# A fourth tile of attention features, new forms of the transfers that fill it, and an earlier second batch

## What is computed

```
mod = (silu(c) @ wmod) -> sa, ca, ga, sb, cb, gb      # per batch; ga, gb: size at least 0.25
h   = layernorm(x) * (1 + ca) + sa
q, k, v = split(h @ qkv_w.T + qkv_b);  q, k = rope(q), rope(k)
attn = softmax(causal(q k^T / sqrt(8)));  o = attn v
x = x + ga * (o @ proj_w.T + proj_b)
h = layernorm(x) * (1 + cb) + sb
y = relu(h @ W_fc.T)^2 @ W_proj.T
x = x + gb * spikes(y) / 5        # how many of 5 thresholds y is over
```

## Time and profile before

| | |
|---|---|
| device time, median of 3 runs | 444.27 us (440.36 to 444.5) |
| the profiled execution | 443.15 us |
| its span (first to last instruction) | 441.4 us |
| TensorE busy / VectorE busy / ScalarE busy | 390.9 / 329.3 / 256.8 us |
| mean granted TensorE clock, share of full speed | 0.988 |

### The profile page before, as it was taken

The page is one execution under the profiler, slowest core; times in us unless marked ns, Lnnn a source line. Parts: engine busy times, 40 slices in busy tenths (PEclk is TensorE's granted clock), DMA queues, the critical chain, the costliest instruction groups (busy, mean ns, idle before and its releaser), DMA issues.

```text
span 441.4 us, 15622 instructions
## 1 busy us (share of the span) xinstructions
PE 390.9 (89%) x6599; PEld 253.1 (57%) x6599; DVE 329.3 (75%) x730; ACT 256.8 (58%) x447; POOL 126.1 (29%) x163
## 2 busy tenths in 40 slices
PE   2778899888999989998899999998998889988885
PEld 2327555555656755666457654765566646753653
DVE  6659995886886988878986997699866777541176
ACT  8203465565676756765666665766665457566523
POOL 6714310430343043503342234304330220040020
PEclk9989999999999999999999999999999899998999
DMA  7056363243314233242415251323233050011001
GB/s 214 22 161 169 99 218 88 70 116 102 104 45 119 75 101 93 80 122 49 137 50 139 64 138 48 117 72 99 67 113 86 16 146 6 25 45 27 3 1 49
DMA packets 26050, 38.53 MB, mean 87 GB/s; under 512 B 5796, under 2 KB 20716, under 8 KB 23692
## 3 DMA queue, kind: packets, MB, share of 16 engines
q1 hardware_dynamic: 25980, 37.53, 29.8%
HBM read 26.35 MB, written 8.65 MB: 79 GB/s over the span
## 4 chain that ended last, share of the span: by engine, by line
PE 41%; DMA 18%; DVE 13%; ACT 10%; POOL 6%; issue 5%; SPq 5%; ACTq 0%; POOLq 0%; DVEq 0%
PE o_bank L611 10%; DMA kf<-k_scr 9%; PE d_bank L528 7%; DVE negmax L978 6%; PE t_bank L593 6%; PE s_bank L548 5%; DMA rden<-r_scr 4%; ACT probs L827 4%; PE a_bank L528 3%; DMA r_scr<-rden_c 2%; POOL parts L1303 2%; PE s_bank L528 2%; SPq L440 2%; PE t_bank L528 2%; POOL o_n L1325 2%
## 5 line engine op out<-in xcount | busy, mean ns | idle before, releaser
L978 DVE TENSOR_REDUCE negmax<-s_bank 128x1 f32<-128x512 f32 (+7 forms) x368 | 192.9, 566 | 56.9 <-PE s_bank L554 54.6
L827 ACT ACTIVATE probs<-t_bank 128x512 f32<-128x512 f32 x288 | 163.0, 594 | 89.8 <-PE t_bank L598 84.5
L548 PE MATMUL s_bank<-kf,qf 126*64 126x512 bf16 (+7 forms) x1024 | 118.7, 293 | 11.8 <-DMA kf<-k_scr 6.2
L593 PE MATMUL t_bank<-qf,kf 128*64 128x512 bf16 (+7 forms) x1024 | 113.3, 290 | 10.8 <-ACT probs L827 9.8
L611 PE MATMUL o_bank<-probs,v 128*32 128x512 f32 (+7 forms) x1024 | 75.1, 412 | 0.0
L548 PEld LDWEIGHTS s_bank<-kf,qf 126*64 126x64 bf16 x1024 | 50.6, 111 | 40.6 <-DVE negmax L978 19.9
L554 PE MATMUL s_bank<-causal,identb 128*64 128x64 bf16 x1024 | 72.6, 195 | 0.0
L598 PE MATMUL t_bank<-causal_t,identb 128*64 128x64 bf16 x1024 | 64.8, 195 | 0.0
L593 PEld LDWEIGHTS t_bank<-qf,kf 128*64 128x64 bf16 x1024 | 41.4, 110 | 35.1 <-ACT probs L827 14.4
L598 PEld LDWEIGHTS t_bank<-causal_t,identb 128*64 128x64 bf16 x1024 | 48.1, 111 | 9.3 <-issue 0.2
L554 PEld LDWEIGHTS s_bank<-causal,identb 128*64 128x64 bf16 x1024 | 47.1, 112 | 8.3 <-issue 8.1
(11 more groups left out here) (145 smaller groups left out, 455.9 us busy)
## 6 DMA issues: line engine op xcount, KB each, us to landing
qf<-q_scr SPq DMA_DIRECT2D x15, 576.0 KB
kf<-k_scr SPq DMA_DIRECT2D x45, 192.0 KB
q_scr<-parts SPq DMA_DIRECT2D x24, 128.0 KB, 1.7
k_scr<-parts SPq DMA_DIRECT2D x24, 128.0 KB, 1.7
xa<-in_x SPq DMA_DIRECT2D x8, 256.0 KB, 3.9
o_t<-o_raw SPq DMA_DIRECT2D x60, 32.0 KB, 2.4
rden<-r_scr SPq DMA_DIRECT2D x15, 128.0 KB
out_y<-count SPq DMA_DIRECT2D x7, 256.0 KB, 6.7
```

Source lines behind the costliest of these rows:

```text
L548: nc.tensor.matmul(bank[C * a:C * (a + 1), col:col + keys], qf[0:KS, slot, 2 * p + a, C * i:C * (i + 1)], kf[0:KS, slot, 2 * p + a, 0:keys ...
L593: nc.tensor.matmul(bank[C * a:C * (a + 1), col:col + w], kf[0:KX, slot, 2 * p + a, C * kb:C * (kb + 1)], qf[0:KX, slot, 2 * p + a, C * kb: ...
L827: nc.scalar.activation(probs[:, v, :], t_bank[u % 2][:, :], ACT.Exp, scale=SCALE).then_inc(e_done, 1)
L978: last = nc.vector.tensor_reduce(own[:, i, p:p + len(same)], cols, AX.X, ALU.max, negate=True)
```

## The change

**Features.** `RING` is 4. To make room, `rest` lives in `rot_s`, `sq` in `relu` (squares in place), the modulation's weights in `relu`, the row of ones in `count`. The order of the 72 rows changes: key part j now fills rows 24j to 24j+23, three copies of its 8 features, so that a key DMA needs only one part; the queries' 24 rows are repeated as a whole. In the sources the copies (3) become the outermost dimension. SyncE issues an even half batch's queries and its key parts 0 and 1 (`some=(0, 2)`) at the end of the batch before, ahead of the third key part's store; the third key DMA follows that store.

**First part.** Batch 1's statistics, the gates' sizes and its normalisation stand before batch 0's rotations; both rotations of batch 1 stand ahead of all maxima; the values' matmuls of batch 1 stand before the scores; one warming of 4 x 512 columns goes, one of 2 x 256 comes. The ones beside the values are set by two memsets of 64 partitions, without selects. SyncE stores batch 1's key parts before the first maxima rows and spread 2.

**Slots.** PROJ goes from slot 16 to 17; the second reciprocals from 10 to 9, the residual from 18 to 19 (not in the last batch).

```diff
-RING = 3
+RING = 4
-D_AT = {16: PROJ, 25: T2, 27: FC, 29: FC + 1, 31: FC + 2, 33: FC + 3}
+D_AT = {17: PROJ, 25: T2, 27: FC, 29: FC + 1, 31: FC + 2, 33: FC + 3}
...
                 q_rows = q_scr[b % 2].rearrange("i (d h) c -> (i d) h c", h=H)[:, heads]
                 sp.dma_start(qf[0:FR, n % RING, own],
-                             q_rows.unsqueeze(1).to_broadcast([NPART * HD, NPART, many, SEQ])).then_inc(done, 16)
+                             q_rows.unsqueeze(0).to_broadcast([NPART, NPART * HD, many, SEQ])).then_inc(done, 16)
...
-                sp.wait_ge(k_stored, 16 * Q_STORES * (b + 1))
-                k_rows = k_scr[b % 2].rearrange("j (d h) c -> d j h c", h=H)[:, :, heads]
                 m = HD * NPART
-                for i in range(NPART):
-                    sp.dma_start(kf[m * i:m * (i + 1), n % RING, own], k_rows).then_inc(done, 16)
+                first, last = (0, NPART) if some is None else some
+                sp.wait_ge(k_stored, 16 * (Q_STORES * b + (2 if last < NPART else Q_STORES)))
+                for j in range(first, last):
+                    k_rows = k_scr[b % 2, j].rearrange("(d h) c -> d h c", h=H)[:, heads]
+                    sp.dma_start(kf[m * j:m * (j + 1), n % RING, own],
+                                 k_rows.unsqueeze(0).to_broadcast([NPART, HD, many, SEQ])).then_inc(done, 16)
...
             for b in range(NB):
                 if 0 < b < final:
                     store_part(b + 1, 1, 2)
-                if 0 < b < final:
-                    spread(2 * b + 2)
+                    spread_keys(2 * b + 2, some=(2, NPART))
...
                 if b + 2 < NB:
                     store_part(b + 2, 1, 1)
+                    spread_queries(2 * b + 4)
+                    spread_keys(2 * b + 4, some=(0, 2))
...
-            keep_warm(t_bank[1], SEQ, 4)
             a_task(1, T1)
             keep_warm(t_bank[1], 256)
             a_task(1, QK)
             gates_out_of_columns()
             a_task(1, QK + 1)
+            a_task(1, V_)
+            keep_warm(t_bank[1], 256, 2)
...
-                    if at == (8 if b == final else 10):
+                    if at == (8 if b == final else 9):
                         reciprocals(b - 1, 1)
-                    if at == 18:
+                    if at == (18 if b == final else 19):
                         residual1(b - 1)
```

More of the change, by code:

```diff
@@ L212, in adaln_kernel @@
         whole = sb("whole", [P, 2, SEQ])
-        rest = sb("rest", [P, 2, SEQ])
+        rest = rot_s
         parts = sb("parts", [P, 2, NPART, SEQ], BF16)
@@ L241, in adaln_kernel @@
         relu = sb("relu", [P, NF, SEQ])
-        sq = sb("sq", [P, NF, SEQ])
+        sq = relu
+        wmod_sb = relu[:, 0:2, :].rearrange("p i c -> p (i c)")[:, 0:6 * P]
         count = sb("count", [P, 2, SEQ])
+        ones_row = count[0:MR, 0, 0:SEQ // 2].bitcast(BF16)
         y_sb = count[:, 1, :].rearrange("p (t d) -> p t d", d=D)
@@ L466, in _ @@
             sp.wait_ge(ones_made, 1)
-            sp.wait_ge(zeros_made[2], 2)
+            for slot in (2, 3):
+                sp.wait_ge(zeros_made[slot], 2)
             sp.dma_start(kf[KS:KX].rearrange("r s h c -> r (s h) c"),
@@ L472, in _ @@
             sp.dma_start(g_scr, gate_t[:, :]).then_inc(gates_stored, 16)
-            for j in range(NPART):
-                store_part(1, 0, j)
+            for qk in range(2):
+                for j in range(NPART):
+                    store_part(1, qk, j)
             place_first_maxima(0)
[L476 to L479, removed]
+            spread(2)
             place_first_maxima(1)
@@ L900, in _ @@
             modulate1(0)
-            for j in range(2):
-                take_part(0, 0, j)
+            take_part(0, 0, 0)
             place_values(0)
+            take_part(0, 0, 1)
             modulate1(1)
+            clear(3, qf)
             act.wait_ge(d_ready, SETUP_TASKS)
             nc.scalar.copy(gate_t[:, :], d_bank[0:3 * NB, 0:P]).then_inc(gates_out, 1)
+            clear(3, kf)
             take_part(1, 0, 0)
@@ L1089, in gates @@
                 last.then_inc(mod_step, 1)
+            def gates():
                 dve.wait_ge(d_ready, 2)
@@ L1126, in _ @@
             normalise1(0)
+            statistics1(1)
+            gate_sizes()
+            normalise1(1)
             dve.wait_ge(wqk_loaded, 16 * 2)
@@ L1138, in _ @@
                 rotary(1, 0, step)
-            for k in range(NS_FIRST):
-                maxima(k)
             for step in range(3):
                 rotary(1, 1, step, bank=d_bank)
-            for k in range(NS_FIRST, scores_ahead(-1)):
+            for k in range(scores_ahead(-1)):
                 maxima(k)
@@ L1350, in _ @@
             for a in range(2):
-                ones = v32[:, :, :, 16 + HD * a:16 + HD * (a + 1)].rearrange("p k g d -> p (k g) d")
-                nc.gpsimd.memset(ones, 1.0).then_inc(v_cleared, 1)
-                pool.wait_ge(v_cleared, 2 + a)
-                last = nc.gpsimd.affine_select(out=ones, in_=ones, pattern=[[0, 2 * NC * NP], [0, HD]], fill=0.0,
-                                               compare_op=ALU.is_ge, base=(C - 1, -C)[a],
-                                               channel_multiplier=(-1, 1)[a])
-            last.then_inc(v_placed_ones, 1)
+                ones = v32[C * a:C * (a + 1), :, :, 16 + HD * a:16 + HD * (a + 1)].rearrange("p k g d -> p (k g) d")
+                nc.gpsimd.memset(ones, 1.0).then_inc(v_placed_ones, 1)
+                pool.wait_ge(v_placed_ones, a + 1)
+            deviation1(1)
             rotary_sum(0, 0)
@@ L1360, in _ @@
             left(0, 0, 2)
-            deviation1(1)
             for qk in range(2):
@@ L1365, in _ @@
                 left(1, qk, 2)
-                split_first_maxima(qk)
+            for pairs in range(2):
+                split_first_maxima(pairs)
             for b in range(NB):
```

17 lines of the change are left out of this document (6 added, 11 removed).

## The result

The changed kernel takes 580.15 us (median of 4 runs, 579.72 to 581.34), the kernel before 443.42 us in the same session. The ratio is 1.310, 95% interval 1.303 to 1.318: 31% slower. The forecast was 570. The engines' own work has hardly changed, as the page shows (busy time by engine, then the chain of work that ended last, by engine).

What follows compares the result with a forecast made beforehand. TensorE was taken to bound the long middle, busy 44.2 of 48 us. From 443 us, +28 in the first part and +98 over six periods gave 569, stated as 570 us; the range ran from below 529 to 675 us.

Steps and rivals of the forecast that it cites:

- Three engines: Query and key spreads: with 3 copies outermost, each spread DMA runs on three engines, all the same three; forecast chance 0.71.
- The first rival: Spreads: the repeated dimension is passed over, 12 and 8 engines stay, and the kernel gets faster, 433 us; chance 0.10.
- the first part: Before the middle: slower spreads cost 24.9 us plus 3 for the clock, +28; the rearrangement's 4.8 lie beside these waits.
- the fourth tile: Odd spreads: it frees their issue from slot 18; with quick spreads, about 3 us less waiting on odd keys.
- S = 16.4 us: Time S of one 1.18 MB spread on three engines at 24 GB/s each, in place of 6.9 us.
- the upper rate: Spreads: 25.4 GB/s an engine, as the gate rows move; the forecast stood near it, with 15.5 us as bound.
- the second rival: Spreads: three engines at the lower rate, 16.5 GB/s each, 23.8 us a spread, 687 us in all; chance 0.10.
- The period: Long middle, one batch: 27.2 + 2S = 60.0 us, 63.0 with the clock, from 46.65; six batches give +98 us.
- The clock: After each of a middle batch's two long waits: 3 us at half rate, 1.5 us lost, 3 us a batch.
- The last third of the keys: Even spread: issued after the queued store, T0 (queries' issue) + 1.7 + 5/6 S + 0.3, then 1.7 + S/6 more.
- The third rival: Middle: three engines, but the fourth tile hides the odd spreads; only first part and even waits paid, 529 us; chance 0.08.
- The projection's slot: Output projection one slot later: neither gain nor loss in the new state, bounds -5 and 0; about -2 with quick spreads.

Runs made afterwards that it cites:

- e3: The kernel before with only the two spreads' sources changed to 3 copies outermost: 586.78 us, one run.
- e1: The changed kernel with the spreads' old sources (24 query rows, 8 key features outermost) and each spread issued whole where it was before: 430.64 us, ratio 0.979.
- e4: The changed kernel, three engines kept, with the third key part's store ahead of the even spread, which is issued whole behind it: 569.42 us, ratio 1.293.
- e8: e1 with projection, reciprocals and residual back at slots 16, 10 and 18 and the rotation waiting for the whole again: 437.04 us, ratio 0.993.
- e7: e1 with three tiles of features (RING = 3) in place of four: 431.2 us, ratio 0.980.
- e9: The kernel before with only three slots moved (projection 17, reciprocals 9, residual 19): 436.71 us, ratio 0.987.
- e10: e8 with the output projection alone at slot 17: 431.73 us, ratio 0.975.
- e2: The changed kernel, its order of issues kept, with 8 features outermost so all six transfers of a spread run on eight engines: 450.45 us, ratio 1.023.
- e6: The changed kernel with queries on twelve engines (three transfers, 24 rows outermost), keys still on three: 490.43 us, one run.
- e5: The edits of e2 and e4 together, eight engines and the store ahead of the even spread, on the changed kernel: 436.59 us, ratio 0.989.

## Why the prediction was right

**Three engines: shown.** The step on which all hung was that 3 copies as the outermost dimension leave three engines. The share of 0.18 shows it, e3 shows that this edit alone makes the loss, and e1 that nothing is left of it once the sources and the order of issues are put back; the order alone is 1.8% (e4). The rule of the Trainium skill (DMA: Bandwidth & Descriptors, Rules for kernel authors) holds here as written, for sources in DRAM too. The first rival (433 us) fell by the share of 0.18. On what the rest of the change is worth its sum was right by luck: e1 is 9.5 us under the kernel before by medians, against the 10 given, but where the rival had 4.8 for the first part, 3 for the fourth tile and 2 for the projection, the runs show some 3 (e8), 0 (e7) and 5 to 8.

**S = 16.4 us: near.** The odd spread's issue and use lie 302.59 - 284.12 = 18.5 us apart, S = 16.8 after the 1.7 of a landing. At 26 GB/s an engine the upper rate of the earlier trace rows was the right neighbour, not the 16.5 GB/s of the eight key engines: the second rival (687 us) falls.

**The period: right in kind, 2.4 us short.** Predicted 63.0, measured 65.4 on average and 66.2 in the one that begins at 251.84. Step by step in that one:

| step | predicted | measured |
|---|---|---|
| even issue to even use | 20.1 | 273.22 - 251.84 = 21.4 |
| even use to odd issue | 8.2 + 1.5 for the clock | 284.12 - 273.22 = 10.9 |
| odd issue to odd use | 18.1 | 302.59 - 284.12 = 18.5 |
| odd use to next issue | 13.6 + 1.5 for the clock | 318.05 - 302.59 = 15.5 |

The waits of TensorE came out at 9.4 and 6.9 us where 8.2 and 6 stood. Two terms were mis-sized.

*The clock.* It stays at 0.50 for 5.7 us after the even wait (273.2 to 278.9) and for 3.6 us after the odd one (302.6 to 306.2), half of each lost, 4.6 us in this batch. The record carried over the one stretch of 3 us in the earlier trace rows to every wait. The stretches differ, and not with the length of the wait: 3.0 us at 0.50 after the longest wait of all (12.0 us, 142.78 to 145.76), 6.2 us after one of 6.3 us (235.17 to 241.32). Over all six batches the loss is 4.2 us each, 1.2 more than the 3 forecast.

*The last third of the keys.* SyncE gets past the queued store at 267.72; the recorded sum, T0 + 1.7 + 5/6 S + 0.3 from 251.84, gives 267.5, so that wait was right. From there the keys take 273.22 - 267.72 = 5.5 us to their use, where 1.7 + S/6 = 4.4 stood. The DMA share is 0.07 from 266 to 268 us and 0.00 from 268 to 269: the engines have run dry by the time the last third is issued. What the whole arrangement costs is 2.3 us a batch (e4) where the record had "some 1 us a batch" for the queueing. SyncE also stands for 13 us and issues none of the outputs' moves, but that cost TensorE nothing here: it has no wait for o_n left.

**The first part: right.** Predicted +28 (24.9 and 3 for the clock), measured +26.4. The first scores for exponentials stand at 62.82 (62.6 predicted), slot 9 at 81.49 (80.9), spread 3 at 106.52 (105.0). The waits in these rows add up to 27.4 us. One cause was not in the record: SyncE's issues themselves became long there (last section), so that the second batch's stores went out late and did not only land late. That the sum came out near all the same is in part luck. That the 5 us of the rearranged first part lie beside the waits fits this; without the waits (e1) the first scores for exponentials come 2.2 us earlier and the maxima row 65.72 - 62.08 = 3.6 us earlier, less than the 4.8 that I gave. e8 with the old slots has the first part and the fourth tile, which is worth nothing (e7), and stands 0.7% (3 us) under the kernel before.

**The fourth tile hides nothing.** The third rival (529 us) falls by the odd waits of 6.3 to 7.1 us in each batch of the middle. And its worth with quick spreads, 3 us in the record, is 0 by e7. TensorE waits for kf 2.5 us with three tiles and 3.7 with four. The row that I had halved, 6.2 us in six waits, shrinks to 2.3 us already when only the projection's slot, the reciprocals' and the residual's are moved (e9).

**The projection's slot: the bound, not the middle.** The record gave it -5 to 0, and 2 us in the first rival. With quick spreads it is worth 5 to 8 us (e9, with the two other slots, against the kernel before; e10 against e8), so the whole wait of the earlier trace rows was gain. I had taken off 3 us for late third keys pushing the outputs' chain back, which e1, with no store queued behind a spread, no longer has to pay. That is how I read the difference; no run has the queued store with twelve and eight engines.

**The sum** was 569 us, the profiled execution took 581.3 (a span of 579.6). Of the 12 us, 14 are missing in the six periods (18.75 and not 16.35 each), and 2 were too many in the first part.

## What to carry to other kernels

Before a DMA's source is rewritten, read its outermost dimension: a repeat written first can take a transfer from 12 engines to 3 though bytes and rows are the same, and a window's DMA share says at once how many engines work. A small store that a later transfer waits for goes ahead of big transfers in the same queue: it cost 2.3 us a batch here with three engines and with eight. Where a bundle of edits gives a few us, run them one at a time: here one number in a table carried most of the gain, and the edit that took most code none.

## What the runs showed of the hardware

**Issues became long behind transfers on three engines.** I had counted an issue at 0.4 to 0.8 us. With three engines at work, SyncE's issues themselves became long, though what they issue is no larger:

```profile
31.70 3.28 SPq L428 DMA_DIRECT2D kf<-k_scr  x3
35.10 2.67 SPq L478 DMA_DIRECT2D kf<-count  x1
37.81 7.36 SPq L392 DMA_DIRECT2D xa<-in_x  x1
45.21 9.09 SPq L482 DMA_DIRECT2D g_scr<-gate_t  x1
54.35 1.49 SPq L400 DMA_DIRECT2D q_scr<-parts  x3
```

In e1 the same load of x is issued in 0.49 us and the gates' store in 0.47. So behind the 2.4 MB of the first two spreads SyncE stood 16 us in two issues, and the second batch's stores went out at 54.35 and not at 36.56. The long issues go with the number of engines: e3 and e4, on three, have the same long issues (4.91 and 9.47 us; 7.36 and 9.23), e2, on eight, has 0.43 and 0.47, and e6, with the keys alone on three, 0.47 and 9.71. That they wait for room behind what is queued is my reading; no run varied how much is queued.

**The rate of one DMA engine differs with the transfer.** 25.4 GB/s on sixteen engines, 20.5 on twelve, 16.5 in the key transfers on eight (18.6 in those of e1, 149 GB/s at the same share), 26 on three. So by these rates a spread goes from 6.9 us, an estimate from the earlier trace rows, to 16.8, a factor of 2.4, and not the 3.2 that the counts alone give (590 kB over 12 and 590 kB over 8 against 1.18 MB over 3). Why eight engines do no better each wasn't tried.

**How long the clock stays low does not follow the wait.** After the twelve long waits of the middle the granted clock stood at 0.50 for between 2.9 and 6.2 us, while TensorE was busy again; the longest wait (12.0 us) was followed by one of the shortest stretches (3.0 us). A forecast can use their mean here, 4.2 us after each wait, half of it lost; one row of such a stretch doesn't give it.

**The price of the queued store did not shrink with the wait for it.** The same reorder gave 2.3 us a batch with three engines (e4) and with eight (e5), where SyncE stood for the store 13.1 and 6.8 us. The percentages, 1.8 and 3.4, differ more than the periods and the spans (12.5 and 13.2 us) do.
